# Attend products of a transformer phase on 64x32 instead of 64x64 tiles of TensorE

## The reference

```python
sim = jnp.einsum('bhwie,bhwje->bhwij', bq, bk2) * QK_SCALE
sim = jnp.where(mask, -jnp.finfo(sim.dtype).max, sim)
attn = jax.nn.softmax(sim, -1)
out = jnp.einsum('bhwij,bhwje->bhwie', attn, bv2)
```

## Time and profile before

| what | value |
|---|---|
| time, median of 3 runs | 4227.32 us (4221.27 to 4227.56) |
| span of the profiled execution | 4218.7 us |
| PE busy | 4055.8 us (96%), 63,591 matmuls |
| PEld busy | 2950.4 us (70%), 63,591 weight loads |
| DVE busy | 3292.4 us (78%) |
| ACT busy | 2422.2 us (57%) |
| POOL busy | 2231.4 us (53%) |
| instructions in all | 144,433 |

### The profile page before, as it was taken

One profiled execution on the slowest core, in us unless ns is written; L12 is line 12 of the kernel. 1 busy time (PEld: TensorE's weight loads), 2 busy tenths in 40 slices (PEclk: granted clock), 3 DMA queues, 4 the chain that ended last, 5 costly groups with the idle time before them and its releaser, 6 DMA issues.

```text
span 4218.7 us, 144433 instructions
## 1 busy us (share of the span) xinstructions
PE 4055.8 (96%) x63591; PEld 2950.4 (70%) x63591; DVE 3292.4 (78%) x6966; ACT 2422.2 (57%) x4410; POOL 2231.4 (53%) x1352
## 2 busy tenths in 40 slices
PE   5999999887999999999999999999999999999997
PEld 4767777564777777777777777777777777777765
DVE  5345354457888988889888898888888888899995
ACT  3111101244767767667776677677667776776664
POOL 2010010025666666666666666666666666666663
PEclk8999999998999999999999999999999999999999
DMA  4111111001111111111111111111111111111110
GB/s 156 41 61 41 56 46 41 21 2 30 40 37 36 48 49 43 41 36 46 51 43 40 37 46 51 42 37 41 46 46 47 38 41 46 46 47 41 40 38 27
DMA packets 76614, 186.14 MB, mean 44 GB/s; under 512 B 16203, under 2 KB 45014, under 8 KB 71510
## 3 DMA queue, kind: packets, MB, share of 16 engines
q1 hardware_dynamic: 75254, 176.51, 13.6%
q10 hardware_dynamic: 736, 0.40, 0.0%
HBM read 61.25 MB, written 2.36 MB: 15 GB/s over the span
## 4 chain that ended last, share of the span: by engine, by line
PE 67%; DVE 5%; ACT 3%; issue 1%; POOL 1%; DMA 0%; POOLq 0%; DVEq 0%; SPq 0%
PE pQ L1690 15%; PE pTO L1723 9%; PE pS L1674 9%; PE pM L1758 7%; PE pM L1747 7%; PE pTO L1736 7%; PE pC L1792 6%; PE pTO L1704 3%; PE pC L1802 3%; ACT sq L1555 2%; ACT pS L1539 1%; DVE rot L1404 1%; DVE m L1408 1%; DVE n L1419 1%; POOL rot L1322 1%
## 5 line engine op out<-in xcount | busy, mean ns | idle before, releaser
L1322 POOL TENSOR_TENSOR rot<-rot,m 128x1024 f32<-128x1024 f32 x384 | 906.4, 2360 | 385.7 <-DVE m L1408 385.7
L1314 POOL TENSOR_TENSOR rot<-rot,rn 128x1024 f32<-128x1024 f32 x384 | 733.7, 1911 | 280.6 <-DVE rn L102 280.6
L1555 ACT ACTIVATE sq<-pQ 128x1024 f32<-128x1024 f32 x380 | 390.1, 1027 | 437.0 <-PE pQ L1690 436.8
L1331 POOL TENSOR_TENSOR E<-E,rc 128x512 f32<-128x512 f32 x384 | 401.2, 1045 | 346.0 <-DVE rc L1394 345.7
L1723 PEld LDWEIGHTS pTO<-PT,V 64*64 64x64 f32 x24576 | 401.5, 134 | 108.9 <-issue 100.2
L1404 DVE TENSOR_TENSOR rot<-pQ,tabl 128x1024 f32<-128x1024 f32 x380 | 456.9, 1202 | 12.1 <-ACT sq L1555 10.0
L1408 DVE TENSOR_TENSOR m<-pQ,tabl 128x1024 f32<-128x1024 f32 x380 | 461.4, 1214 | 0.0
L1419 DVE TENSOR_REDUCE n<-sq 128x16 f32<-128x1024 f32 x380 | 459.3, 1209 | 0.0
L1674 PEld LDWEIGHTS pS<-kT,qT 64*32 64x32 f32 x24576 | 360.9, 107 | 136.6 <-issue 101.7
L1723 PE MATMUL pTO<-PT,V 64*64 64x32 f32 x24576 | 443.5, 221 | 4.3 <-ACT PT L1564 2.8
L1674 PE MATMUL pS<-kT,qT 64*32 64x64 f32 x24576 | 424.9, 218 | 21.9 <-issue 12.5
(11 more groups left out here) (231 smaller groups left out, 6939.8 us busy)
## 6 DMA issues: line engine op xcount, KB each, us to landing
V<-V SPq DMA_DIRECT2D x192, 384.0 KB, 3.5
b_cB<-b_crow SPq DMA_DIRECT2D x32, 1024.0 KB, 5.9
xs<-XT SPq DMA_DIRECT2D x192, 64.0 KB, 2.9
V<-V SPq DMA_DIRECT2D x96, 128.0 KB, 3.3
ys<-XT SPq DMA_DIRECT2D x192, 64.0 KB, 2.0
wq<-in_wqkv SPq DMA_DIRECT2D x6, 512.0 KB, 4.4
wk<-in_wqkv SPq DMA_DIRECT2D x6, 512.0 KB, 4.2
wv<-in_wqkv SPq DMA_DIRECT2D x6, 512.0 KB, 5.4
```

The source lines that it names most:

```text
L1314: e.tensor_tensor(r, r, rn[b % 2][:, c:c + HEADS].unsqueeze(2).to_broadcast([P, HEADS, HD]), ALU.mult)\
L1322: e.tensor_tensor(rot[j % RING][:, :], rot[j % RING][:, :], m2[:, :, :].rearrange("p h d -> p (h d)"), ALU.add)\
```

## The change

Each call in `attend` becomes two: the 64 channels of a head's values are split into two halves of 32 columns, each on its own tile of 64 rows and 32 columns. The column position `c` takes the four values 0, 32, 64 and 96 instead of 0 and 64, and each half writes its 32 partitions of the same PSUM region. The streamed operand is the same 32 columns of `PT` for both halves. Nothing else is changed; the semaphore is raised by the last call as before.

```diff
                     for j in range(4):
                         h = 4 * g + j
-                        c = HD * (j % 2)
-                        x = e.matmul(pOV[b % 2][c:c + HD, j // 2, w // 4, WIN * (w % 2):WIN * (w % 2 + 1)],
-                                     V[n % 2][r:r + KEYS, w // 4, 1 - w % 2, h * HD:(h + 1) * HD],
-                                     PT[i % 2][r:r + KEYS, (b // 2) * P + 32 * j:(b // 2) * P + 32 * j + 32],
-                                     start=True, stop=True, tile_position=(r, c))
+                        for d in (0, HD // 2):
+                            c = HD * (j % 2) + d
+                            x = e.matmul(pOV[b % 2][c:c + HD // 2, j // 2, w // 4, WIN * (w % 2):WIN * (w % 2 + 1)],
+                                         V[n % 2][r:r + KEYS, w // 4, 1 - w % 2, h * HD + d:h * HD + d + HD // 2],
+                                         PT[i % 2][r:r + KEYS, (b // 2) * P + 32 * j:(b // 2) * P + 32 * j + 32],
+                                         start=True, stop=True, tile_position=(r, c))
                 x.then_inc(p_pv.sem, 1)
```

## The result

The changed kernel takes 4720.02 us (median of 4 runs, 4711.81 to 4744.98) against 4225.47 us for the kernel before on the same chip: a ratio of 1.1185, 95% interval 1.1155 to 1.1216. The forecast was 4506 us, with a range of 4340 to 4680. The direction was right; the loss is 495 us where 279 were forecast, and the time lies outside the range. The profiled execution of after is the slowest of the four and spans 4743.0 us, 524 us more than that of before; the comparison of the two traces goes by these 524, not by the 495 of the medians.

A forecast was written before the change was run, and what follows sets the result against it. PE's order was taken to bound the kernel: 321 us of packet stops, less 14.8 us already present and 27 us at the edges, gave +279 us on 4227.3, so 4506 us; own range 4405 to 4670, widened to 4340 to 4680.

The forecast's parts named there:

- What bounds it: Transformer phase: PE is busy 796.08 of 800 us, so whatever lengthens PE's order lengthens the kernel.
- issue: PE waits the profile does not explain, read as waiting for instruction packets: 14.8 us before, 250 to 400 us forecast after.
- The packets: PE's instruction queue: 24,576 more pairs (weight load plus matmul) outrun packets of 126.4 pairs; 321 us of stops forecast.
- the slide: Packet edge moved over all positions of a pass to sum PE's stops: 347 us, scaled to 321 us.
- C: Shortest time between two instruction packets for PE, taken as 3.3 us; 3.7 us as the upper end.
- The edges: Where scores and attend meet, both on 64x32 afterwards: 0.28 us a pass saved, 27 us in all.
- The stream: Attend: 128 records of 27 ns, four at a time, if issued every 7 ns; no change from 0.94 us taken.
- The clock: Dry PE dropping its clock was taken as nothing, from the stop at 1793.8 in a stretch at clock 1.00.
- two at a time, or slower issue: Attend: a pair keeps its 17 ns, so attends last 1.9 us with 181 us of stops; 4727 us, chance 0.15.
- The rivals on the other side: Whole kernel: packets no limit, 4200 us, chance 0.06; no difference, stops mostly covered, 4227 us, chance 0.02.

The follow-up runs named there:

- e2: Only attends 0 and 1 split into two halves, attends 2 and 3 left as in the kernel before; 4370.58 us.
- e5: The changed kernel with project(A, 0) moved ahead of scores(B, 0) and project(A, 1) ahead of attend(Dn, 3); 4697.95 us.
- e7: The changed kernel with 16 instead of 32 streamed columns of PT in each attend matmul; 4718.56 us.
- e6: The kernel before with project(A, 0) moved ahead of scores(B, 0) and project(A, 1) ahead of attend(Dn, 3), nothing else; 4458.61 us.
- e1: The changed kernel with only the first of the two 64x32 halves computed, 64 pairs an attend as before; 4150.97 us.
- e10: The kernel before with one PE wait a pass, between combine and probs 0, for a small DMA; 4449.85 us.

## Why the prediction was wrong in its size

*What bounds it* was right: PE's order is the kernel's time, and no wait for another engine came up in after (the first after "issue" is 2.5 us).

*The packets* were right. 321 us were forecast from the slide with C = 3.3 us, in some 200 stops, "worst behind scores 1 and attend 2"; the trace has 311 us in 222 stops, and 296 of them in the attend and the scores. The value of C can be read directly in after: of the 651 packets of this queue in the phase none starts less than 3.23 us behind the one before it. That fits packets of 16 KiB that come one at a time, as the stop of the earlier trace rows suggested, and every stop of after ends 1.15 to 1.60 us after one. That the sum came within 10 us of the rows is in part luck: in e2 and e5 the same slide, scaled in the same way, was 28 and 21 us over. And the slide reckons from start to start but was scaled to the idle rows, which leave out the ends of the matmuls ahead; from start to start the stops are 362 us after and 19 before, 343 more where 306 were forecast. The page Runtime: NRT & Kernel Launch of the Trainium skill ("Instruction fetch mechanics"), by which such fetching is mostly hidden, is contradicted once more by the 222 stops.

*The edges* were right: -0.28 us a pass was forecast for the two places where scores and attend meet. With the stream of their attends 0.16 us longer, these stretches grew by only 0.06 and 0.03 us, so the edges gave back some 0.10 and 0.13 us, 0.23 a pass (22 us; 27 were forecast).

*The stream* was mis-sized, though little. I took no change of 0.94 us; it is 1.10 us, 0.16 x 384 = 61 us. The step held that 7 ns a pair, seen over four pairs, go on; over 128 they are 8.6 ns. e7 shows that these are not the streamed columns, so the reckoning by columns (27 ns, four at a time) was the wrong model, even where it came near. The page TensorE: Matmul & The Clock Gate of the Trainium skill ("Wait — 56ns, not 53.3ns?") with its 25 ns from start to start is again not borne out: 8.6 ns here.

*The clock* is the step that failed: "That a dry PE drops its clock I take as nothing". It rested on one stop, 1.30 us long, in a stretch whose clock is 1.00. That row was read rightly and did not carry that far: the stops of before are 1.3 us at most, and those that the slide forecast behind scores 1 and attend 2 were 2 us on average. After has 304 us more at half clock, which is up to 152 us. The traced execution lost 245 us more than forecast (524 for 279): up to 152 for the clock, 61 for the stream, 5 for the edges and 37 for the stops from start to start are 255. The 152 are an upper bound. A rival of the same size as the sum itself, a drop of the clock behind each forecast stop, could have been priced from rows: a project of 1.72 us that takes twice as long behind each of 200 stops is 344 us at the upper end.

*The rival "two at a time, or slower issue"* gave 4727 us, almost the time measured, and by its signs it is wrong: it wanted attends of 1.9 us and 181 us of stops, and the trace has 1.10 us and 311 us. A sum that hits the time does not confirm its terms. The rivals on the other side fell: "issue" did not stay at 15 us.

No kernel here that computes everything beats the kernel before. The stops of before, which the order of e6 does remove, are worth 15 us and cost more to move than they hold.

## What to carry to other kernels

Splitting small matmuls over more tiles can free the array and starve the engine: count the instructions that a dense stretch takes in the time that one packet of instructions needs (here 126 pairs in 3.3 us), and slide that length over the order of the groups. Where the order is dense already, a stop has to be priced twice, as time without work and as the groups behind it at the lower clock; judge the second price by the length of the forecast stops and by the groups around them, not by the stops in the old trace. Splitting two attends of the four costs 151 us in one place and 354 us in another, so look first at what stands next to the place that is changed.

## What the runs showed of the hardware

Three things I had not expected. The price of a small pair differs by its tile and does not fall with the columns that it streams: 8.5 to 8.6 ns on 64x32 with 16 or 32 columns (9.8 ns in e1, on two of the four column positions), but 14.9 ns on 64x64 with 32 columns and 18 to 19 ns with 16, in two different orders; the last is open. The clock fell behind 20 of 28 stops of 1.6 to 1.8 us between groups on small tiles (after), and behind 1 of 60 between groups on 128x128 tiles (e10). And packets of instructions never followed each other closer than 3.2 us in any of the kernels, while PE was dry for up to 3.2 us at a time (after) and resumed 1.15 to 1.60 us after the end of one.
